# Attention scores of batches 2 to 15 by seven block products in place of eight, in a layer of attention and a gated feed-forward net

## What is computed

```python
qkv = jnp.einsum('bnd,ed->bne', t, W_qkv) + b_qkv          # D_M = D_K = D_V = 256
scores = jnp.einsum('bqd,bkd->bqk', Q, K) / jnp.sqrt(jnp.float32(D_K))
attn = jax.nn.softmax(scores, axis=-1)
return jnp.einsum('bqk,bkv->bqv', attn, V)
...
h = jax.nn.silu(gate) * up                                  # HIDDEN = 768
return jnp.einsum('bsh,dh->bsd', h, wd)
...
x = x + _layernorm(_L0_attn_ref(_layernorm(x, axis=-1), L0_attn_W_qkv, L0_attn_b_qkv), axis=-1)
x = x + _layernorm(_L0_ffn_ref(_layernorm(x, axis=-1), L0_ffn_w_gate, L0_ffn_w_up, L0_ffn_w_down), axis=-1)
```

## Time and profile before

| what | value |
|---|---|
| median of 3 runs | 1362.18 us (1361.79 to 1363.02) |
| span of the profiled execution, first to last instruction | 1359.9 us |
| around that span, against the median | 2.3 us |
| TensorE busy, matmuls | 1344.6 us (99%), 7378 |
| VectorE, ScalarE, GpSimd busy | 903.6, 877.1, 831.5 us |
| granted TensorE clock, mean | 0.999 |
| one pass of the loop | 83.1 us |

### The profile page before, as it was taken

One profiled execution on the slowest core, in us unless ns is written; L12 is line 12 of the kernel. 1 busy time (PEld: TensorE's weight loads), 2 busy tenths in 40 slices (PEclk: granted clock), 3 DMA queues, 4 the chain that ended last, 5 costly groups with the idle time before them and its releaser, 6 DMA issues.

```text
span 1359.9 us, 22330 instructions
## 1 busy us (share of the span) xinstructions
PE 1344.6 (99%) x7378; PEld 722.2 (53%) x7378; DVE 903.6 (66%) x2167; ACT 877.1 (65%) x1378; POOL 831.5 (61%) x1001
## 2 busy tenths in 40 slices
PE   8999999999999999999999999999999999999998
PEld 5445455555555555555554555545555455555555
DVE  7895675766766666666766656667575676756666
ACT  6765775666757577575675756667666675755654
POOL 5686483765837648376484755748466584754554
PEclk9999999999999999999999999999999999999999
DMA  6996482845638366392753836548374574725411
GB/s 182 184 195 136 87 152 81 140 102 111 132 89 154 73 128 139 71 169 66 133 134 71 162 79 123 126 86 148 86 133 108 104 137 102 132 63 104 106 29 67
DMA packets 432968, 157.24 MB, mean 116 GB/s; under 512 B 413905, under 2 KB 416337, under 8 KB 432850
## 3 DMA queue, kind: packets, MB, share of 16 engines
q1 hardware_dynamic: 432048, 154.99, 55.7%
q10 hardware_dynamic: 802, 0.79, 0.2%
HBM read 36.70 MB, written 16.78 MB: 39 GB/s over the span
## 4 chain that ended last, share of the span: by engine, by line
PE 88%; DVE 3%; POOL 2%; DMA 2%; SPq 2%; issue 1%; ACT 1%; DVEq 0%; ACTq 0%; POOLq 0%
PE S L868 88%; DMA yTl<-yl 1%; SPq L276 1%; DVE S L768 1%; POOL xl L368 1%; DVE st L777 1%; POOL Pl L386 1%; DVE mxs L739 0%; POOL yl L413 0%; SPq L257 0%; DVE st L721 0%; ACT Ph L518 0%; POOL rs L331 0%; POOL xs L356 0%; DMA xs<-in_L_attn_t 0%
## 5 line engine op out<-in xcount | busy, mean ns | idle before, releaser
L511 ACT ACTIVATE P<-S,nmx,sc 128x1024 f32<-128x1024 f32 x128 | 153.6, 1200 | 269.8 <-DVE nmx L743 267.6
L386 POOL TENSOR_TENSOR Pl<-P,Ph 128x1024 f16<-128x1024 f32 x96 | 205.5, 2142 | 47.3 <-issue 30.3
L739 DVE TENSOR_REDUCE mxs<-S 128x1 f32<-128x1024 f32 x128 | 156.1, 1219 | 115.3 <-PE S L868 115.2
L805 DVE SCALAR_TENSOR_TENSOR hf<-S,sc,hf 128x512 f32<-128x512 f32 x192 | 141.9, 746 | 132.5 <-ACT hf L546 126.6
L868 PE MATMUL S<-PTh,xh 128*128 128x512 f16 x512 | 194.1, 379 | 0.0
L868 PE MATMUL S<-PTl,xh 128*128 128x512 f16 x512 | 194.0, 379 | 0.0
L868 PE MATMUL S<-PTh,xl 128*128 128x512 f16 x512 | 194.0, 379 | 0.0
L868 PE MATMUL S<-xTh,zTh 128*128 128x512 f16 x506 | 191.8, 379 | 2.0 <-ACT P L511 1.0
L868 PE MATMUL S<-xTl,zTh 128*128 128x512 f16 x508 | 192.5, 379 | 0.0
L868 PE MATMUL S<-xTh,zTl 128*128 128x512 f16 x508 | 192.5, 379 | 0.0
L422 POOL TENSOR_TENSOR hTl<-hf,hTh 128x512 f16<-128x512 f32 x128 | 146.1, 1156 | 50.2 <-ACT hTh L553 43.9
(11 more groups left out here) (155 smaller groups left out, 2478.8 us busy)
## 6 DMA issues: line engine op xcount, KB each, us to landing
xs<-in_L_attn_t SPq DMA_DIRECT2D x32, 512.0 KB, 5.3
X<-in_L_attn_t SPq DMA_DIRECT2D x32, 512.0 KB, 4.6
out_x<-X SPq DMA_DIRECT2D x62, 256.0 KB, 2.9
PTh<-Ph SPq DMA_TRANSPOSE x128, 3.2
PTl<-Pl SPq DMA_TRANSPOSE x128, 3.3
hTl<-in_L_ffn_w_gate SPq DMA_DIRECT2D x1, 768.0 KB, 6.6
hTh<-in_L_ffn_w_up SPq DMA_DIRECT2D x1, 768.0 KB, 8.3
hTl<-in_L_ffn_w_down SPq DMA_DIRECT2D x1, 768.0 KB, 10.2
```

The source lines that it names most:

```text
L386: p.engine.tensor_tensor(out=Pl[:, m % 3, :], in0=P[:, m % 2, :], in1=Ph[:, m % 3, :], op=ALU.subtract).then_inc(pl_vector if i in PL_ON_V ...
L511: a.engine.activation(P[:, m % 2, :], ps[:, bank:bank + 2, :].rearrange("p a n -> p (a n)"), ACT.Exp, bias=nmx[:, c:c + 1], scale=sS, accu ...
L739: v.engine.tensor_reduce(mxs[:, c:c + 1], ps[:, bank:bank + 2, :].rearrange("p a n -> p (a n)"), axis=AX.X, op=ALU.max, negate=True).then_ ...
L805: v.engine.scalar_tensor_tensor(out=hf[:, n % 3, :], in0=ps[:, bank + 1, :], scalar=sc2[:, 4:5], in1=hf[:, n % 3, :], op0=ALU.mult, op1=AL ...
```

## The change

For batches 2 to 15 the scores are made in pairs of query blocks (rows e = 2p and o = 2p + 1) against the two halves of the keys, with the two halves dj of the 256 numbers as the inner dimension. That is a 2 by 2 by 2 block product, and the changed kernel makes it with seven block products in place of eight (Winograd's form of Strassen's scheme). It needs sums and differences of the operands' blocks and of the products:

- `mix_keys` (VectorE, once a batch): four `tensor_tensor` on `xs`, 128x4x128 each, each behind the one before it. `t_high`, `t_low` and four transposing DMAs (`turn_t`) make `tTh` and `tTl` of them.
- `mix_queries` (VectorE, for each g): four `tensor_tensor` on `zw`, 128x2x128 each. `q_high` and `q_low` make `qTh` and `qTl`.
- Products M1 to M7, three matmuls each: `pair_first` makes M1 (bank 0), M2 (bank 1), M4 (bank 3) and M5 (bank 2); `pair_second` adds M6 onto bank 0, `pair_third` adds M7 onto it, and `pair_last` adds M3 onto bank 2. ScalarE copies bank 0 to `P` after M1, after M6 and after M7 (`copy_m1`, `copy_u2`, `copy_u3`).
- `sum_21`, `sum_22`, `sum_11`, `sum_12` (VectorE) add a bank and a half row of `P`, write the sum to `P` and take the row maximum in the same call. `row_max` is gone in these batches, and `exp` reads `P` in SBUF, not PSUM. `P` has four slots for two.
- The lists of all engines are written anew. `XS` (the scale of x) goes from 2^11 to 2^9 with constants that follow from it.

```diff
-        P = sb("P", [128, 2, N])
+        P = sb("P", [128, 4, N])
...
+        def t_low(p, b, g):
+            n = 2 * (b - 2) + g
+            p.wait_ge(th_done, n + 1)
+            p.wait_ge(mix_x, 4 * (b - 1))
+            p.wait_ge(tl_turned, 16 * n)
+            p.engine.tensor_tensor(out=tl[:, :, :], in0=xs[:, 4 * g:4 * g + 4, :], in1=th[:, :, :], op=ALU.subtract
+                                   ).then_inc(tl_done, 1)
...
+        def mix_queries(e, b, g):
+
+            w = zw[:, :, :].rearrange("p j (u h n) -> p j u h n", h=2, n=128)
+            a11, a12, a21, a22 = w[:, 0, :, 1, :], w[:, 1, :, 1, :], w[:, 0, :, 0, :], w[:, 1, :, 0, :]
+            n = 4 * (2 * (b - 2) + g)
+            zl_wait(e, b, g, 1)
+            e.engine.tensor_tensor(out=a22, in0=a22, in1=a21, op=ALU.add).then_inc(mix_z, 1)
+            e.wait_ge(mix_z, n + 1)
+            e.engine.tensor_tensor(out=a21, in0=a21, in1=a11, op=ALU.subtract).then_inc(mix_z, 1)
+            e.wait_ge(mix_z, n + 2)
+            e.engine.tensor_tensor(out=a11, in0=a22, in1=a11, op=ALU.subtract).then_inc(mix_z, 1)
+            e.wait_ge(mix_z, n + 3)
+            e.engine.tensor_tensor(out=a12, in0=a12, in1=a11, op=ALU.subtract).then_inc(mix_z, 1)
...
+        def copy_u2(a, b, p):
+            n, m = 4 * (b - 2) + p, 8 * b + 2 * p + 1
+            a.wait_ge(m6_out, n + 1)
+            p_free(a, m)
+            a.engine.activation(P[:, m % 4, 512:1024], ps[:, 0, :], ACT.Copy).then_inc(u2_copied, 1)
...
+        def sum_max(v, out, bank, other, least, most):
+            return v.engine.tensor_tensor_reduce(out=out, in0=ps[:, bank, :], in1=other, scale=1.0, scalar=least, op0=ALU.add,
+                                                 op1=ALU.max, accum_out=most)
...
+        def pair_second(t, b, p):
+            t.wait_ge(m1_copied, 4 * (b - 2) + p + 1)
+            product(t, 0, (qTh, qTl, 0), (tTh, tTl), slice(4, 8), 1, 2 * p + 1, True).then_inc(m6_out, 1)
+
+        def pair_third(t, b, p):
+            t.wait_ge(u2_copied, 4 * (b - 2) + p + 1)
+            product(t, 0, (qTh, qTl, 0), (tTh, tTl), slice(4, 8), 0, 2 * p, True).then_inc(m7_out, 1)
+
+        def pair_last(t, b, p):
+            t.wait_ge(c22_done, 4 * (b - 2) + p + 1)
+            product(t, 2, (qTh, qTl, 1), (xTh[b % 2], xTl[b % 2]), slice(4, 8), 1, 2 * p + 1, True).then_inc(m3_out, 1)
```

More of the change, by code:

```diff
@@ L1654, in _ @@
-            silu(a, 14, 0, 1, 0)
-            silu(a, 14, 0, 2, 2)
-            h_high(a, 14, 0, 0)
-            h_high(a, 14, 0, 1)
-            silu(a, 14, 0, 3, 6)
+            y_hat(a, 14, 1, 0)
+            h_high(a, 14, 0, 0)
+            silu(a, 14, 0, 1, 0)
+            y_hat(a, 14, 1, 1)
+            silu(a, 14, 0, 2, 2)
+            h_high(a, 14, 0, 1)
+            y_high(a, 14, 1)
+            silu(a, 14, 0, 3, 6)
+            exp(a, 15, 6)
+            add_bias(a, 13, 1, 0)
+            p_high(a, 15, 6)
@@ L1906, in _ @@
[L1906 to L1914 removed]
+                x_stats(v, b + 3, 1)
+                sum_11(v, b + 2, 0)
+                row_inverse(v, b + 1, 1)
+                sum_21(v, b + 2, 0)
+                d_add(v, b, 0, 1)
+                sum_22(v, b + 2, 0)
@@ new lines, in _ @@
+                sum_21(v, b + 2, 3)
+                sum_22(v, b + 2, 3)
+                x1_add(v, b + 1, 1, 0)
+                x1_add(v, b + 1, 1, 1)
+            sum_12(v, 14, 3)
+            z_float(v, 15, 0, 0)
+            h_mul(v, 13, 0, 0, 6)
+            mix_keys(v, 15)
+            row_inverse(v, 14, 0)
+            mix_queries(v, 15, 0)
+            h_mul(v, 13, 0, 1, 2)
+            h_mul(v, 13, 0, 2, 6)
+            h_mul(v, 13, 0, 3, 0)
+            d_stats(v, 12, 1, 1)
+            h_low(v, 13, 0, 2)
@@ L1953, in _ @@
-            row_inverse(v, 15, 0)
-            d_stats(v, 13, 0, 1)
-            d_add(v, 13, 0, 1)
-            o_low(v, 14, 1, 1)
-            row_max(v, 15, 5, 2)
-            p_low(v, 15, 4)
-            row_max(v, 15, 6, 0)
-            y_scale(v, 14, 1, 0)
-            y_stats(v, 14, 1, 0)
-            y_scale(v, 14, 1, 1)
-            y_stats(v, 14, 1, 1)
-            h_mul(v, 14, 0, 0, 6)
-            h_mul(v, 14, 0, 1, 0)
-            x1_add(v, 14, 1, 0)
+            p_low(v, 14, 4)
+            mix_queries(v, 15, 1)
@@ new lines, in _ @@
+            sum_21(v, 15, 0)
+            d_stats(v, 13, 0, 1)
+            sum_22(v, 15, 0)
+            o_low(v, 14, 0, 0)
+            sum_11(v, 15, 0)
+            sum_12(v, 15, 0)
+            row_inverse(v, 14, 1)
+            o_low(v, 14, 0, 1)
+            d_add(v, 13, 0, 1)
+            y_scale(v, 14, 0, 0)
+            y_scale(v, 14, 0, 1)
+            y_stats(v, 14, 0, 0)
+            y_stats(v, 14, 0, 1)
+            sum_11(v, 15, 1)
+            x1_add(v, 14, 0, 0)
+            x1_add(v, 14, 0, 1)
@@ L1967, in _ @@
+            x1_add(v, 14, 1, 0)
+            x1_add(v, 14, 1, 1)
+            sum_21(v, 15, 3)
+            sum_22(v, 15, 3)
+            p_low(v, 15, 4)
+            h_mul(v, 14, 0, 0, 6)
+            sum_12(v, 15, 3)
+            h_mul(v, 14, 0, 1, 0)
+            d_stats(v, 13, 1, 0)
+            d_stats(v, 13, 1, 1)
             h_mul(v, 14, 0, 2, 2)
             h_mul(v, 14, 0, 3, 6)
-            x1_add(v, 14, 1, 1)
-            row_max(v, 15, 7, 2)
-            h_mul(v, 14, 0, 4, 0)
+            d_add(v, 13, 1, 0)
@@ L2077, in second_part @@
+            project_v(t, 1, 1, (x1_done, 10), (x1_done, 12))
+            pair_second(t, 2, 3)
+            pair_third(t, 2, 3)
+            project_z(t, 3, 0, 0, (u3_copied, 4), (c11_done, 4))
+            pair_last(t, 2, 3)
+            gate_up(t, 1, 0, 0, 6, (ol_done[0], 4), (ol_done[1], 4), three)
+            down(t, 0, 1, 0, (x1_done, 14), three)
+            for b in range(1, 13):
+                gate_up(t, b, 0, 1, 2, (c12_done, 4 * b), (c21_done, 4 * b), three)
                 gate_up(t, b, 0, 2, 6, (silu_done, 12 * b + 1), (hmul_done, 12 * b + 1), three)
+                gate_up(t, b, 0, 3, 0, (zw_done, 4 * b + 9), (zw_done, 4 * b + 10), three)
```

1433 lines of the change are left out of this document (822 added, 611 removed).

## The result

The changed kernel takes 1487.62 us (median of 4, 1483.73 to 1491.93) against 1362.37 us beside it: ratio 1.092, 95% interval 1.0895 to 1.0946. It is 125 us slower; I had said 1447, in a range up to 1472. The span of the profiled execution, which is the fastest of the four, is 1481.7 us, 121.8 more than before. The four runs lie 8 us apart, so that differences to this kernel are good to some 4 us.

What follows compares the result with a forecast made beforehand. TensorE's matmuls were taken to bound the kernel. 1359.9 - 36.3 (matmuls) + 23.5 (copies) + 13 x (3.0 + 4.5) (port waits) = 1444.6 us of span; with 2.3 us to the median, 1447 us, range 1348 to 1472.

Steps and rivals of the forecast that it cites:

- Matmuls, 36.3 us: TensorE, 14 batches: seven products for eight save 168 matmuls of 0.216 us, 36.3 us, 2.59 a pass.
- Copies of bank 0: Fourth pair: TensorE loses 0.84 us at ScalarE's copy twice a pass, 23.5 us in all; other pairs' copies hidden.
- Sums: VectorE, replacing row_max: sixteen sums a batch at 0.75 plus 0.1 us, 4 us more, covered by idle VectorE.
- Mixes and the port: Gate part: two-input VectorE mixes each wait for a whole GpSimd instruction, holding TensorE at two places; mix_keys caught once, hidden.
- first place: Chunk 5 of gate_up: TensorE waits 3.0 us a pass for h_mul of chunk 3, behind mix_queries.
- second place: attend behind mix_queries of g = 1: waits of 5.4 us against 1 us of slack, taken as 4.5 a pass.
- the sum itself: Whole span: 1359.9 - 36.3 + 23.5 + 13 x (3.0 + 4.5) = 1444.6 us.
- the signs of being wrong: Profile after: among them, TensorE's clock falling in the new pauses would make the prediction wrong; no size given.
- Rest: Transposing DMAs, GpSimd's t_low and q_low: covered, though making the collisions denser; first two batches and last cost nothing.
- The one called worse: Rival: delay goes on into the attention part through x_stats, sums and pair_last; 2 us a pass more, 1475 and above; chance 0.07.
- Port free: Faster rival: VectorE finds the port free or waits stay within slack; only copies left, 1349 us; chance 0.24.

Runs made afterwards that it cites:

- e13: In a reordered variant of the changed kernel (1408.95 us), the four mixes of g = 0 alone became reductions with one SBUF input: 1378.16 us.
- e14: Changed kernel with the four mixes of g = 1 alone replaced by reductions with one SBUF input: 1406.76 us.
- e5: Changed kernel with only the lists of the first two batches reordered (a load, statistics of batch 1): 1484.37 us.
- e1: Changed kernel with all twelve mixes of a batch replaced by reductions with one SBUF input, mixing left out: 1377.87 us.
- e15: Reordered variant of the changed kernel (1410.53 us) with all twelve mixes of a batch replaced by reductions with one SBUF input: 1375.92 us.
- e6: Changed kernel with mix_queries of g = 1 behind h_mul of chunk 5, p_low of block 4 kept early, q_high and q_low later: 1419.73 us.
- e2: Changed kernel with h_low and h_mul of g = 1 ahead of mix_queries and p_low of block 4, q_high behind p_high of block 7: 1460.37 us.
- e7: e6 with mix_queries of g = 0 moved to where mix_keys stood, mix_keys behind z_float of g = 1, t_high and t_low later: 1450.94 us.

## Why the prediction was wrong, and where it was right

*Matmuls, 36.3 us*: right; 168 fewer, 0.216 us apart where nothing waits.

*Copies of bank 0, 0.84 us twice a pass*: right. Gaps of 0.85 and 0.94 us (waits of 0.69 and 0.78), nothing at the other pairs.

*Sums, 0.75 + 0.1 us, hidden*: right, 0.69 to 0.75 + 0.08. TensorE waits for them 1.5 us in all 13 passes.

*Mixes and the port*: the mechanism and both places were right. `mix_keys` is caught once, in its fourth instruction (median 1.68 us for 0.69), and hidden, as predicted. The sizes were not right. By e13 and e14 the places cost 2.0 and 5.8 us a pass, clock included, 7.8 for my 7.5, but that is luck: the first place was too large in my sum and the clock was not in it at all.

*The steps that failed.* The 13 passes are 100.5 us longer together (1180.6 for 1080.1), where my terms, -2.59 + 1.68 + 7.5 each, give 85.7. The gaps and the distances at half clock, added up over all 13 passes, show where each term went:

| term, 13 passes together, us | predicted | in the traces |
|---|---|---|
| seven products for eight | -33.7 | -33.7 |
| two copies of bank 0 (once `xTl` ended later) | 21.8 | 23.8 |
| first place | 39.0 | 23.9 |
| second place | 58.5 | 56.6 |
| matmuls at half clock | nothing | 28.4 |
| wait for yTl (2.8 for 3.2 before) | nothing | -0.4 |
| all other small waits | nothing | 4.3 |
| work that the new list puts behind `project_z(15, 0)` | nothing | -2.4 |
| sum | 85.7 | 100.5 |

The first failed step is the sum itself, which prices the waits at both places and puts TensorE's clock at nothing. The clock stood only under the signs of being wrong, and it fell: 26.8 us behind the second place and 1.6 at the start. The second is the 3.0 us of the first place, where the gap is 1.8 to 2.3. In the pass from 557.18 us TensorE comes there 23.7 us after the end of `project_v`, as counted (23.6), but the mixes end at 23.4 for 24.3 and `h_mul` of chunk 3 at 25.6 for 26.6: `y_low` starts at 16.7 for 17.5, and the rest moves with it.

The third is the sentence in "Rest" that the first two batches and the last cost nothing. Their matmuls are kept, but not their lists. `project_z(2, 0)` starts at 109.8 us for 97.0, 12.8 later, and from `project_z(15, 0)` to the end it takes 191.3 us for 182.8. With the saving of that part, -0.9 in my sum, this is 9.4 us more; 2.4 of them are the work moved there, and the first place comes once more, with a gap of 2.5 us. 14.8 + 12.8 + 9.4 = 37 us is what the span lies above my 1444.6; the rest is between span and median, 5.9 us for 2.3, since the profiled execution is the fastest of four.

*The start.* Of the 12.8 us 4.8 are there by the third group of matmuls of batch 0's z (at 23.4 for 18.6), with a wait of 2.9 us for `xTl`; with one load and two statistics out of the way (e5), `project_z(2, 0)` starts 3.8 us earlier. 3.8 more are gaps ahead of the first two `attend` (5.8 for 2.0). 3.6 are the gap at `project_z(2, 0)` itself:

```profile
109.79 0.38 PE L1026 MATMUL S<-xTh,Ah 128*128 128x512 f16 x1 [3.48 <-issue]
```

The profile puts this wait down to nobody, but the list does not: ahead of it TensorE waits for `ffn_turned`, the six transposing DMAs of the feed-forward weights. The last of them, in the changed kernel and then in the kernel before:

```profile
104.14 1.83 SPq L340 DMA_TRANSPOSE Ul<-X  x1
```

```profile
84.23 1.72 SPq L311 DMA_TRANSPOSE Wl<-hf  x1
```

In all sixteen traces of the changed kernel and its variants `project_z(2, 0)` starts 5.5 to 5.7 us after the issue of this DMA, wherever that is (98.2 to 105.3 us); before, it starts 12.8 us after it and without a wait. So it is this DMA, later in the queue's new order, that TensorE waits for there. No kernel was run in which it alone is changed back, and the last 0.5 us are not accounted for.

*Rivals.* The one called worse named a time of 1475 and above, and the time is there, but by another way: no delay in `x_stats` or `pair_last` held TensorE, and sums did for 1.5 us. "Port free" was not met in the kernel, and its 1349 us was wrong too: e1 and e15 give 1376 to 1378. e1's span lies 27.6 us above that rival's sum: 11.8 are the start, 5.1 the end (2.4 of them the moved work), and 10.7 are in the 13 passes, above all gaps at `attend` (6.5 together), at the copies (3.6 more than 21.8) and tenths elsewhere. With them that rival would have been on the slower side.

One reading of the prediction is wrong without effect: the longest wait of TensorE before is 2.1 us, once at the start, not 1.6.

## What to carry to other kernels

A product saved is worth its matmuls only as far as no new wait comes with it; here 2.6 us a pass were saved, and the two copy round trips (1.8) and small waits of tenths took them back before the mixes cost anything (e1). Where dependent two-input instructions on VectorE stand beside a queue of ready two-input work on GpSimd, count one whole GpSimd instruction for each link, and ask first whether the work can be had with one SBUF input. In a schedule with three engines at 65 to 78% beside TensorE at 91%, a wait taken away by reordering mostly comes back one buffer further on: of the seven orders, one (e6) kept most of what it freed.

When a diff rewrites the lists outside the loop, price these too, the DMA queue's with them: start and end were 21 of the 122 us. And a term added up over all passes says more than the waits of one: the pass shown above has a wait for y that ten of twelve do not have.

## What the runs showed of the hardware

The ten waits of 4.9 us on TensorE cost 2.1 to 2.6 us more each, since the matmuls behind them run at the lower of the two clocks, and 18 matmuls without use in the gap save 28.5 us. The stretch with the wait of 1.64 us (668 to 672) shows a clock of 1.00. Between these the length of the wait does not decide: in e2 the wait of 3.19 us at 690.53 has 0.76 behind it (692 to 696), and an equal one in the same kernel has 1.00:

```profile
869.17 0.39 PE L1177 MATMUL S<-tTh,qTh 128*128 128x512 f16 x1 [3.18 <-ACT P L592]
```

```profile
871.00:875.00 4.00, 4.00 (x20) 1.76 (x19) 2.13 (x7) 3.89 (x9) 3.83 (x4) 1.00 0.46 89
```

The two waits of 2.61 us in the changed kernel have 0.80 and 0.71 behind them, and the one of 3.26 us in e7 has 0.75. And a reduction with one SBUF input runs beside GpSimd's two-input subtraction at its full pace, 0.42 us for 256 elements, where an addition or subtraction of two took up to 2.23 at the same place.
